# Attention scores in a cross-attention kernel: four matmuls over 154 key columns with mixed high and low parts of Q in place of three over 308

## The reference, cut to what matters

```python
# B=32 sequences, T=512 rows of x, S=77 keys, D=512, 16 heads of 32; all float32
qh = split_heads(q @ wq.T + bq)            # q = x
kh = split_heads(k @ wk.T + bk)            # k = v = ctx
vh = split_heads(v @ wv.T + bv)
scores = einsum('ntd,nsd->nts', qh, kh) / sqrt(32)
scores = scores + mask * PAD
ctx = einsum('nts,nsd->ntd', softmax(scores), vh)
out = layernorm(merge_heads(ctx) + q) * gamma + beta
```

## Time and profile before

| | |
|---|---|
| median of 3 runs | 1153.81 us (1152.42 to 1155.73) |
| profiled execution | 1157.28 us, span of the trace 1155.5 us |
| mean granted TensorE clock | 0.988 |
| busy share PE / PEld | 97% / 90% |
| busy share DVE / ACT / POOL | 71% / 53% / 67% |
| DMA | 122 GB/s over the span |

### The profile page before, as it was taken

How to read it: one execution, slowest core, us unless ns; L and a number is a source line. 1 busy time by engine, 2 the same in 40 slices (tenths; PEclk the granted TensorE clock), 3 DMA queues, 4 the chain that set the end, 5 groups by cost and what they waited for, 6 DMA issues and landing times.

```text
span 1155.5 us, 25702 instructions
## 1 busy us (share of the span) xinstructions
PE 1123.1 (97%) x7541; PEld 1037.8 (90%) x7541; DVE 822.1 (71%) x1622; ACT 612.5 (53%) x1008; POOL 771.8 (67%) x667
## 2 busy tenths in 40 slices
PE   7899999999999999999999999999999999999994
PEld 7788789999999999999999999999999999999983
DVE  5776467777777777777777777777777777777786
ACT  3321254556566555555555656655555555565551
POOL 4999523677766676766667776667676666777465
PEclk9999999999999999999999999999999999999996
DMA  7745433233343444343344333344443334333223
GB/s 228 261 147 188 150 104 90 74 122 95 116 119 117 126 126 126 116 120 99 102 123 122 106 105 119 117 126 126 126 116 122 98 102 123 123 101 110 85 82 128
DMA packets 147207, 141.07 MB, mean 122 GB/s; under 512 B 86452, under 2 KB 88004, under 8 KB 147172
## 3 DMA queue, kind: packets, MB, share of 16 engines
q1 hardware_dynamic: 146564, 140.29, 40.1%
q10 hardware_dynamic: 608, 0.33, 0.1%
HBM read 91.71 MB, written 48.85 MB: 122 GB/s over the span
## 4 chain that ended last, share of the span: by engine, by line
PE 84%; DVE 2%; POOL 1%; issue 0%; ACT 0%; DMA 0%; DVEq 0%; SPq 0%; POOLq 0%
PE q_ps L724 31%; PE o_ps L765 23%; PE s_ps L740 18%; PE t_ps L751 12%; POOL x_lo L991 0%; DVE stats L822 0%; DVE attn L853 0%; PE q_ps L765 0%; DVE y L862 0%; DMA xT_raw<-in_xT 0%; DVE attn L814 0%; DVE row_max L885 0%; DVE y L868 0%; ACT q_hi L1030 0%; DVE y L843 0%
## 5 line engine op out<-in xcount | busy, mean ns | idle before, releaser
L765 PE MATMUL o_ps<-v_tiles,pt 128*128 128x66 f32 x2520 | 310.7, 270 | 1.5 <-DVE attn L814 1.5
L765 PEld LDWEIGHTS o_ps<-v_tiles,pt 128*128 128x128 f32 x2520 | 304.0, 192 | 1.9 <-issue 1.9
L885 DVE TENSOR_REDUCE row_max<-s_ps 128x8 f32<-128x616 f32 x256 | 203.2, 794 | 118.2 <-PE s_ps L740 118.1
L740 PE MATMUL s_ps<-bd,q_hi 128*128 128x308 f32 x1024 | 260.5, 305 | 1.1 <-ACT q_hi L1030 1.1
L991 POOL TENSOR_TENSOR x_lo<-xT_raw,x_hi 128x512 fp32r<-128x512 f32 x124 | 159.3, 1286 | 117.8 <-ACT x_hi L1026 117.7
L961 POOL TENSOR_TENSOR attn<-attn,x_rows 128x512 f32<-128x512 f32 x124 | 160.2, 1292 | 115.8 <-DVE attn L814 115.8
L1036 ACT COPY pt<-t_ps 128x512 f32<-128x512 f32 (+1 forms) x320 | 175.0, 588 | 107.1 <-PE t_ps L751 107.0
L1030 ACT ACTIVATE q_hi<-q_ps,bq_col 128x512 fp32r<-128x512 f32 x125 | 86.1, 689 | 254.9 <-PE q_ps L724 254.9
L724 PE MATMUL q_ps<-x_lo,wq_hi 128*128 128x512 f32 x500 | 218.7, 437 | 2.5 <-PEq L142 2.1
L1016 ACT ACTIVATE probs<-probs 128x616 f32<-128x616 f32 x256 | 183.3, 716 | 64.3 <-DVE probs L894 64.3
L894 DVE TENSOR_TENSOR probs<-s_ps,row_max 128x616 f32<-128x616 f32 x256 | 204.6, 799 | 5.7
(11 more groups left out here) (96 smaller groups left out, 1292.9 us busy)
## 6 DMA issues: line engine op xcount, KB each, us to landing
xT_raw<-in_xT SPq DMA_DIRECT2D x128, 256.0 KB, 3.5
x_rows<-in_x SPq DMA_DIRECT2D x32, 1024.0 KB, 5.6
out<-y SPq DMA_DIRECT2D x128, 256.0 KB, 2.1
k_scratch<-k_out SPq DMA_DIRECT2D x8, 1232.0 KB, 5.4
bd<-k_scratch SPq DMA_DIRECT2D x128, 77.0 KB, 2.4
v_scratch<-v_out SPq DMA_DIRECT2D x16, 264.0 KB
v_tiles<-v_scratch SPq DMA_DIRECT2D x256, 9.9 KB
ctx_raw<-in_ctxT SPq DMA_DIRECT2D x3, 1232.0 KB, 6.2
```

Source lines behind the costliest of these rows:

```text
L740: mm = pe.matmul(s_ps[t % 2][:, j, 0:GS], (q_hi, q_lo)[u][:, g, P * t:P * t + P], bd[par][:, v, g, :, :].rearrange("p h s -> p (h s)"), st ...
L765: mm = pe.matmul(bank_of(b, t)[:, col:col + tile_cols[i]], pt[h][0:w, i, P * t:P * t + P], v_tiles[v_buffer(b, h)][0:w, i, 0:tile_cols[i]] ...
L885: dve.tensor_reduce(row_max[:, u, :].rearrange("p (j h) -> p j h", j=2), score_heads(t), AX.X, ALU.max).then_inc(max_ready, 1)
```

## The change

The high and low parts of Q are no longer two tiles `q_hi` and `q_lo` but two tiles `q_pair[0]` and `q_pair[1]`. Of a group's four heads, `q_pair[0]` holds heads 0 and 1 alone: their high part on their own partitions 0 to 63, their low part on partitions 64 to 127. `q_pair[1]` holds heads 2 and 3: high part on 64 to 127, low part on 0 to 63. The high part of K is loaded twice into `bd`: on its head's partitions and on the 32 partitions 64 away (the twin); the low part of K stays on the head's own partitions, and its twin partitions stay zero. A matmul of `q_pair[d]` with the high K gives high x high + low x high at once, one with the low K gives high x low. So there are four matmuls of 154 columns (2 heads x 77 keys) per group instead of three of 308. The two matmuls of one d stand one behind the other and name the same weights.

`high_q` and `q_low` become two instructions each, of 64 partitions x 512; those of `q_low` write other partitions than they read. `load_keys` issues eight DMAs instead of four, every other one with 4 runs per partition. The waits count twice as many signals.

```diff
-    KDMA = HG * DMA
+    KDMA = 2 * HG * DMA
+    HP = P // 2
...
-        q_hi = sb(whole, "q_hi", [P, NG, T], F32R)
-        q_lo = sb(whole, "q_lo", [P, NG, T], F32R)
+        q_pair = [sb(whole, f"q_pair{d}", [P, NG, T], F32R) for d in range(2)]
...
                         sp.dma_start(bd[par][rows, :, :, q, :].bitcast(F32), k_dram[b, rows, :, :, :]
                                      ).then_inc(k_loaded[par], DMA)
+                        twin = slice((DH * q + HP) % P, (DH * q + HP) % P + DH)
+                        sp.dma_start(bd[par][twin, 0, :, q, :].bitcast(F32), k_dram[b, rows, 0, :, :]
+                                     ).then_inc(k_loaded[par], DMA)
...
-                        at_least(pe, q_hi_ready, used)
-                        at_least(pe, q_lo_ready, used)
+                        at_least(pe, q_hi_ready, used * 2)
+                        at_least(pe, q_lo_ready, used * 2)
...
                     for j in range(2):
                         g = 2 * h + j
-                        for n, (u, v) in enumerate(terms):
-                            mm = pe.matmul(s_ps[t % 2][:, j, 0:GS], (q_hi, q_lo)[u][:, g, P * t:P * t + P],
-                                           bd[par][:, v, g, :, :].rearrange("p h s -> p (h s)"),
-                                           start=(n == 0), stop=(n == 2))
+                        for d in range(2):
+                            for v in range(2):
+                                mm = pe.matmul(s_ps[t % 2][:, j, 2 * S * d:2 * S * d + 2 * S],
+                                               q_pair[d][:, g, P * t:P * t + P],
+                                               bd[par][:, v, g, 2 * d:2 * d + 2, :].rearrange("p h s -> p (h s)"),
+                                               start=(v == 0), stop=(v == 1))
...
-                def q_low(b, g):
-
-                    dve.wait_ge(q_hi_ready, b * 4 + (g + 1))
-                    dve.scalar_tensor_tensor(out=q_lo[:, g, :], in0=q_bank(b, g)[:, :], scalar=bq_col[:, g:g + 1],
-                                             in1=q_hi[:, g, :], op0=ALU.add, op1=ALU.subtract
-                                             ).then_inc(q_lo_ready, 1)
+                def q_low(b, g, d):
+
+                    rows, twin = slice(HP * d, HP * d + HP), slice(HP - HP * d, P - HP * d)
+                    dve.wait_ge(q_hi_ready, b * 8 + (2 * g + d + 1))
+                    dve.scalar_tensor_tensor(out=q_pair[d][twin, g, :], in0=q_bank(b, g)[rows, :],
+                                             scalar=bq_col[rows, g:g + 1], in1=q_pair[d][rows, g, :],
+                                             op0=ALU.add, op1=ALU.subtract).then_inc(q_lo_ready, 1)
...
                 def high_q(b, g):
                     act.wait_ge(q_done, b * 4 + (g + 1))
-                    act.activation(q_hi[:, g, :], q_bank(b, g)[:, :], ACT.Identity, bias=bq_col[:, g:g + 1]
-                                   ).then_inc(q_hi_ready, 1)
+                    for d in range(2):
+                        rows = slice(HP * d, HP * d + HP)
+                        act.activation(q_pair[d][rows, g, :], q_bank(b, g)[rows, :], ACT.Identity,
+                                       bias=bq_col[rows, g:g + 1]).then_inc(q_hi_ready, 1)
```

More of the change, by code:

```diff
@@ L211, in load_keys @@
                         sp.dma_start(bd0[rows, :, :, q, :].bitcast(F32), k_dram[b, rows, :, :, :]).then_inc(k_loaded[0], DMA)
+                        twin = slice((DH * q + HP) % P, (DH * q + HP) % P + DH)
+                        sp.dma_start(bd0[twin, 0, :, q, :].bitcast(F32), k_dram[b, rows, 0, :, :]).then_inc(k_loaded[0], DMA)
                 def store_values(c, first, end):
@@ L370, in _ @@
                     act.wait_ge(q_done, g + 1)
-                    act.activation(q_hi[:, g, :], k_ps[g][:, :], ACT.Identity, bias=bq_col[:, g:g + 1]
-                                   ).then_inc(q_hi_ready, 1)
+                    for d in range(2):
+                        rows = slice(HP * d, HP * d + HP)
+                        act.activation(q_pair[d][rows, g, :], k_ps[g][rows, :], ACT.Identity, bias=bq_col[rows, g:g + 1]
+                                       ).then_inc(q_hi_ready, 1)
             @block.vector
@@ L466, in _ @@
                 for g in range(2):
-                    dve.wait_ge(q_hi_ready, g + 1)
-                    dve.scalar_tensor_tensor(out=q_lo[:, g, :], in0=k_ps[g][:, :], scalar=bq_col[:, g:g + 1],
-                                             in1=q_hi[:, g, :], op0=ALU.add, op1=ALU.subtract
-                                             ).then_inc(q_lo_ready, 1)
+                    for d in range(2):
+                        rows, twin = slice(HP * d, HP * d + HP), slice(HP - HP * d, P - HP * d)
+                        dve.wait_ge(q_hi_ready, 2 * g + d + 1)
+                        dve.scalar_tensor_tensor(out=q_pair[d][twin, g, :], in0=k_ps[g][rows, :],
+                                                 scalar=bq_col[rows, g:g + 1], in1=q_pair[d][rows, g, :],
+                                                 op0=ALU.add, op1=ALU.subtract).then_inc(q_lo_ready, 1)
             @block.tensor
@@ L939, in step @@
                         if real(a + h) and t % 2 == 1 and not in_phase_one(a + h, g):
-                            q_low(a + h, g)
+                            q_low(a + h, g, 0)
+                            q_low(a + h, g, 1)
                         if rows is not None:
```

10 lines of the change are left out of this document (6 added, 4 removed).

## The result

| | before | changed |
|---|---|---|
| median (4 runs each) | 1154.05 us | 1181.71 us (1179.11 to 1185.87) |
| ratio | | 1.0243, 95% interval 1.021 to 1.0276 |
| profiled execution / span | 1157.28 / 1155.5 us | 1185.87 / 1183.9 us |

The changed kernel is 2.4% slower, by 28 us; forecast were +19 us, in a range that ended at 1191. The direction and the main term, the hand-over, held; some 8 us were not in the sum. The two profiled executions lie 3 and 4 us above the medians.

The account below looks back on a forecast made before the run. PE, busy 97% of the span, was taken to bound the kernel. Scores 2.6 + hand-over 15.5 + phase one 1 = +19 us, profiled 1157.3 to 1176, median 1173 us; range 1155 to 1191.

Parts of the forecast that it names:

- the hand-over: Q's bank at t = 3: PE waits 0.25 us for the second q_lo, 62 times, +15.5 us, between 10 and 17.
- Scores on PE: Eight score matmuls per step, bound by weight loads: +2.6 us at t = 0, 0 where transposes follow.
- the first transpose's load: Behind the scores: if it took 0.108 us as a whole transpose does, 7 us more, the upper bound.
- The gap that the Trainium skill gives: Score matmuls on PE: 67 ns for 154 columns, 0.53 us for eight, 84 us gained over 256 units.
- the high end: Q's bank: second q_lo starts 0.03 us after the first ends, so PE's load is 0.27 us late, 17 us in sum.
- DVE behind it: DVE's queue after q_lo, up to the product's scaling: 0.67 to 0.78 us later, no further wait, margin 0.07 us.
- SP: Four more DMAs before the x loads: at most 3.2 us against 3.5 us of room before the v tiles, cost 0.
- The rest: End of phase one: two more instructions of 0.7 us on ACT and DVE while PE has nothing to do, +1 us.

Follow-up runs that it names:

- e1: Kernel before with only the new score shape, eight matmuls of 154 columns per step, its own Q instructions and K loads: 1158.66 us, ratio 1.0048.
- e4: Changed kernel with the transposes reordered, one transposed tile at t = 2 and two at t = 3: 1166.54 us, ratio 1.0106 to the kernel before.
- e7: Changed kernel with both q_low instructions of phase two reading and writing partitions 0 to 63: 1176.46 us, ratio 1.0189 to the kernel before.
- e2: Changed kernel with Q in halves, but scores again six matmuls of 308 columns and K loaded without twins: 1178.34 us, ratio 1.0208.
- e9: Changed kernel with three score matmuls per group (308, 154, 154 columns), high Q also whole in `q_all`, transposes in old order: 1163.13 us, ratio 1.0062.
- e3: Kernel before with only the four more DMAs per batch that load high K onto its twin partitions: 1154.44 us, ratio 1.0006.
- e10: Kernel before with the transposes reordered as in e4, one tile at t = 2 and two at t = 3: 1157.38 us, ratio 1.0017.
- e5: Changed kernel with eight score matmuls of 76 to 78 columns per step instead of 154: 1187.3 us, one run.
- e6: Changed kernel with eight score matmuls of 232 columns per step instead of 154: 1186.8 us, one run.
- e8: The three score matmuls per group of e9 with the transposes reordered as in e4: 1137.49 us, ratio 0.9848 to the kernel before.

## Why the prediction was right, point by point

- **Scores on PE** (+2.6 at t = 0, 0 elsewhere): right, and for its reason. The stages after, e1 and the two widths show the floor of 0.11 us per load. Measured +3.3 at t = 0, +1.1 elsewhere; e1 has +4.0 in all. The bound that the first transpose's load might add 7 us did not come up; with transposes behind them the scores cost 0.01 us a step.
- **The gap that the Trainium skill gives** for matmuls at full clock, columns / 2.4 + 2.5 ns ("TensorE: Matmul & The Clock Gate", "Back-to-back issue gap"), would have given 84 us less. The same section calls it the gap of an isolated matmul and says that at few columns it counts too little, since it has no term for the weight load; the forecast left that out. The runs with 77, 154 and 232 columns agree with the section: all take 0.11 us a matmul. The estimate from the section "LDWEIGHTS", 0.107 us a load, agrees with 0.112.
- **The hand-over** (0.25 us, 62 times, +15.5): right. Measured 0.27 in 60 steps, +16.1, and e4 takes 15 us of it away. The choice near the high end was right: 0.03 us between the two q_low where the row maximum followed 0.08 before the end. The reason, which was only an inference then, is shown by e7. The rule of the Trainium skill ("VectorE: DVE Perf Modes", "Two Vector instructions with no wait between them": an instruction whose input or output begins in another quarter of the partitions than the last one's starts only when the earlier ones have finished) agrees with it in both directions: held in the changed kernel, not held in e7.
- **DVE behind it** (no further wait, by a margin of 0.07 us): right in what it cost, not in the margin. The forecast moved the scaling by 0.78 us, but the row maximum is held too, which the forecast said beside its sum and did not count in it: the chain from the second q_low to the scaling took 2.31 us instead of 2.15. That uses up the margin, and in 56 of 61 steps at t = 0 the product's load starts only 0.12 us behind the scaling. The cost is small, since the eighth score load delays the product as much anyway: 0.01 of the product's +0.05 us is the wait, 0.04 the load (e1). Without that load, in e2, the wait costs 0.036 us a step, and in e9 0.2.
- **SP** (0): right; eight DMAs of K take 5.8 us instead of 3.2 (610.61 to 616.41 in SP's queue), and e3 measures nothing.
- **The rest** (+1): this term was too small. Measured +7.9 in the profiled executions, of which phase one's end has 1.5, the first steps of phase two 3.7, and the tail 2.7. It belongs to Q in halves: e1's 4.0 us lie in its full steps alone, while e2 has 5 of its 23.7 outside of them and e7 6 of its 20.5. In the first steps there are no products yet to stand between Q and the bank, so the longer hand-over is fully on the path there, and I had priced it for full steps only. One wait for the pair tile, 1.8 us at 146 us, is followed by 3.4 us in which the granted clock is 0.50, the lower of TensorE's levels, where the kernel before kept 1.00. The view by stretches of the changed kernel (stretch and its length; busy time and count of PE, PEld, DVE, ACT, POOL; granted clock; share of the DMA engines; GB/s):

```profile
148.90:152.30 3.40, 3.40 (x12) 2.82 (x11) 2.13 (x3) 1.74 (x3) 1.99 (x2) 0.50 0.04 7
```

That is before's place in the same view:

```profile
148.90:152.30 3.40, 3.38 (x23) 2.90 (x22) 2.22 (x4) 2.72 (x5) 1.95 (x2) 1.00 0.00 0
```

Twelve matmuls in the place of 23 in the same 3.4 us: half of the stretch, some 1.7 us, is lost there. The traces of the experiments tell the two apart. The first steps of phase two take 22.7 to 23.8 us in the four kernels with whole Q (before, e1, e3, e10), 25.1 to 25.4 in e2, e4, e5 and e7, where PE's loads have a like wait for the pair tile (2.0 to 2.5 us, 2.2 in the changed kernel) and the clock stays at 1.00 behind it, and 27.5 in the changed kernel and in e6, which have the low stretch. So some 2 us are the longer hand-over and some 2 the clock; the wait alone doesn't bring the low stretch, and what does is not shown. The tail has one low stretch more than before as well, but by itself it varies by 3 us among the kernels with whole Q (44.0 to 47.0) and by 7 among the others (46.3 to 53.1), so its 2.7 us, like phase one's 1.5, are not secured by one trace each.

## What to carry to other kernels

Here a matmul cost the longer of its moving columns and its weight load (0.11 us), so count loads as well as columns: trading three matmuls of 308 columns for four of 154 gained nothing, three with one wide and two narrow gained 0.16 us of 0.85. When an instruction is delayed, follow everything queued behind it: the scaling at the end of DVE's queue had 0.07 us of room on paper and none on the chip. Before an instruction on ACT or DVE is cut into halves by partitions, look for who waits for its end: half the partitions took the full time (0.75 us on DVE, 0.69 on ACT), and a bank that is read in two instructions is free one instruction later. Where such a hand-over doesn't fit, move independent work of the waiting engine into the gap; here one line, worth nothing by itself, made a slower kernel's idea pay.

## What the runs showed of the hardware that I had not expected

- Two neighbouring matmuls on the same float32r weights load them twice: 8053 loads for 8053 matmuls.
- Between 77 and 232 columns the width of a float32r matmul makes hardly a difference to a sequence of them: 1.29, 1.30 and 1.33 us for eight of them and four transposes.
- A wide matmul (308 columns) and two narrow ones (154) take 0.15 + 0.11 + 0.11 us, each the longer of its columns and a load (e8).
- Two instructions of DVE on different partitions (the two q_low, and the row maximum behind them) lay 0.06 to 0.1 us further apart than the same on partitions that begin alike (e7). On a path that is waited for 60 times, that was 5 us.
